# The maximum of attention as a row of its product, and a first section that starts with x and spreads dt*u by TensorE

## The reference

```python
# selective scan, per direction: u, dt (T x 256), B, C (T x 16)
dA = exp(dt[t, :, None] * A)
h  = dA * h + (dt[t] * u[t])[:, None] * B[t][None, :]
y[t] = einsum("ds,s->d", h, C[t])
# attention, 8 heads on 2 latent groups of 32, causal
p = softmax(q @ k.T * 128**-0.5 + mask)
```

## Time and profile before

| | us |
|---|---|
| median of 3 runs (1987.96 to 1991.94) | 1990.47 |
| profiled execution | 1983.65 |
| its span | 1981.8 |
| PE busy in the span | 1660.5 (84%) |
| DVE busy | 1547.1 (78%) |
| ACT busy | 1120.8 (57%) |
| POOL busy | 754.8 (38%) |

### The profile page before, as it was taken

How to read it: one execution, slowest core, us unless ns; L and a number is a source line. 1 busy time by engine, 2 the same in 40 slices (tenths; PEclk the granted TensorE clock), 3 DMA queues, 4 the chain that set the end, 5 groups by cost and what they waited for, 6 DMA issues and landing times.

```text
span 1981.8 us, 26962 instructions
## 1 busy us (share of the span) xinstructions
PE 1660.5 (84%) x8352; PEld 768.2 (39%) x8352; DVE 1547.1 (78%) x2173; ACT 1120.8 (57%) x1555; POOL 754.8 (38%) x601
## 2 busy tenths in 40 slices
PE   2434487889997999889997899889998999989988
PEld 0210123344443445344443345344443445434545
DVE  1999899869995899769995899869996999641404
ACT  2445387358744786458744786458744785433232
POOL 0345555324533355324533355324533445310102
PEclk8655699899999999899999999999999999989999
DMA  7999999657955687657955787657955686500000
GB/s 197 228 221 225 227 230 210 150 135 181 230 133 141 158 216 178 156 123 183 231 131 140 159 214 181 156 126 181 232 132 141 165 209 184 130 0 0 6 1 6
DMA packets 107915, 309.48 MB, mean 156 GB/s; under 512 B 15970, under 2 KB 32244, under 8 KB 107764
## 3 DMA queue, kind: packets, MB, share of 16 engines
q1 hardware_dynamic: 93556, 279.32, 59.5%
q10 hardware_dynamic: 14208, 28.32, 4.4%
HBM read 287.67 MB, written 19.92 MB: 155 GB/s over the span
## 4 chain that ended last, share of the span: by engine, by line
PE 36%; DVE 21%; ACT 21%; issue 12%; DMA 5%; ACTq 2%; DVEq 1%; SPq 1%; POOL 0%; POOLq 0%
PE ps_pair L698 8%; PE ps_pair L795 7%; DVE sb_hst L1263 7%; ACT L919 6%; PE ps_pair L854 5%; DMA sb_ring<-spread_dram 5%; PE ps_pair L783 4%; PE ps_pair L874 3%; PE ps_pair L651 3%; ACT sb_ring L950 3%; ACT sb_mix L1099 3%; DVE sb_dd L1241 2%; DVE ps_in L1255 2%; DVE sb_nmax L1404 2%; PE ps_pair L798 2%
## 5 line engine op out<-in xcount | busy, mean ns | idle before, releaser
L1532 POOL TENSOR_TENSOR sb_hc<-sb_hst,sb_crep 128x512 f32<-128x512 f32 x512 | 659.3, 1294 | 990.0 <-DVE sb_hst L1263 617.1
L1263 DVE TENSOR_TENSOR_SCAN sb_hst<-sb_ring,ps_in 128x512 f32<-128x512 f32 x512 | 620.5, 1212 | 21.2 <-ACT sb_ring L950 13.2
L950 ACT ACTIVATE sb_ring<-sb_ring,sb_A 128x512 f32<-128x512 f32 x512 | 345.2, 713 | 227.0 <-DMA sb_ring<-spread_dram 99.5
L1255 DVE TENSOR_TENSOR ps_in<-sb_ring,ps_brow 128x512 f32<-128x512 f32 x512 | 354.3, 692 | 22.1 <-DMA sb_ring<-spread_dram 4.7
L854 PE MATMUL ps_pair<-sb_mix,sb_ew 128*128 128x512 f32 x512 | 251.3, 625 | 19.8 <-ACT sb_h L1065 9.4
L919 ACT ACT_TABLE_LOAD x193 | 247.6, 1283 | 7.3 <-DVE sb_xd L1314 3.2
L633 PE MATMUL ps_y<-sb_hc,sb_const 128*32 128x512 f32 x1024 | 154.2, 677 | 83.0 <-POOL sb_hc L1532 59.4
L795 PE MATMUL ps_pair<-sb_g,sb_h 128*128 128x512 f32 x320 | 170.5, 658 | 23.4 <-DVE sb_dd L1243 11.1
L783 PE MATMUL ps_pair<-sb_h,sb_g 128*128 128x512 f32 (+3 forms) x512 | 165.4, 452 | 6.5 <-DVE sb_nmax L1404 3.2
L854 PEld LDWEIGHTS ps_pair<-sb_mix,sb_ew 128*128 128x128 f32 x512 | 96.0, 198 | 156.7 <-issue 87.1
L874 PEld LDWEIGHTS ps_pair<-sb_ew,sb_eh 128*128 128x128 f32 x1024 | 120.6, 192 | 37.3 <-issue 13.6
(11 more groups left out here) (219 smaller groups left out, 2037.9 us busy)
## 6 DMA issues: line engine op xcount, KB each, us to landing
sb_ring<-spread_dram SPq DMA_DIRECT2D x512, 512.0 KB, 5.6
spread_dram<-sb_dd ACTq DMA_DIRECT2D x32, 512.0 KB, 3.0
sb_brep<-cut_dram ACTq DMA_DIRECT2D x16, 256.0 KB, 3.8
sb_crep<-cut_dram ACTq DMA_DIRECT2D x16, 256.0 KB, 4.2
sb_xtok<-in_L_attn_x_dram SPq DMA_DIRECT2D x8, 256.0 KB, 5.1
sb_ew<-in_L_ffn_w_dram SPq DMA_DIRECT2D x2, 1024.0 KB, 8.5
out_dram<-sb_yy ACTq DMA_DIRECT2D x8, 256.0 KB, 2.3
sb_h<-in_L_ffn_h_w_dram SPq DMA_DIRECT2D x1, 1024.0 KB, 7.0
```

The lines of the kernel that those rows point to most:

```text
L950: act.activation(ring[:, n % RING, 0, :], ring[:, n % RING, 0, :], ACT.Exp, scale=A[d][:, g:g + 1]).then_inc(sem["dA"], 1)
L1255: dve.tensor_tensor(ps_in[n % 2][:], ring[:, n % RING, 1, :], ps_brow[:], ALU.mult).then_inc(sem["dbu"], 1)
L1263: dve.tensor_tensor_scan(hst[:, HST_SLOT[n], :], ring[:, n % RING, 0, :], ps_in[n % 2][:], 0.0, ALU.mult, ALU.add).then_inc(sem["scan"], 1)
L1532: pool.tensor_tensor(hc[:, n % 6, :], hst[:, HST_SLOT[n], :], crep[n // NU][:], ALU.mult).then_inc(sem["hc"], 1)
```

## The change

There are three parts, and all written-out orders are new.

**Attention.** The split into bf16 parts, `pick` and the products of line 798 go. `nmax` becomes a zeroed 128-column tile whose columns 0, 32, 64, 96 hold the maxima, in fp32; PE turns it with eight fp32 transposes into the two banks of `ps_pair[0]`, and ACT copies four single lines of it (1 x 1024 each) into a zero-key row of the queries, opposite to a line of ones (four copies of 1 x 512) in `kz`. The queries exist twice for that (`qAB`), one copy for each half. The score product of a round then contains the minus-maximum.

**The start.** x is SP's first load, then 12 loads of first need; the raising of the semaphores comes behind them; nine loads (`ones`: the backward direction and the mask) and 26 later ones follow. The 3 MB of expert weights and the gate's are issued in SECOND, one load after every fourth ring load.

**FIRST.** ACT copies dt*u to `duk`, and PE spreads it to 128 partitions by a 0/1 matrix, one product a unit, into one of g0 to g3; `drive` reads it from there, and B from SBUF. The ring's loads carry the dt half alone, 256 KB. ACT copies ten of the turned weights instead of DVE, and the turned weights use all four banks.

```diff
-            for name in PER:
-                sp.sem_inc(sem[name], first(name))
             with nc.allow_non_contiguous_dma(reason="per-channel vectors, once"):
+                sp.dma_start(xtok[:], a["x"][0:1]....).then_inc(sem["x_in"], 16)
+                for dst, src in loads[:-3]:
+                    sp.dma_start(dst, src).then_inc(w_in, 16)
                 sp.wait_ge(w_zero, 1)
-                for dst, src in loads:
+                for dst, src in loads[-3:]:
                     sp.dma_start(dst, src).then_inc(w_in, 16)
+                for name in PER:
+                    sp.sem_inc(sem[name], first(name))
+                for dst, src in ones:
+                    sp.dma_start(dst, src).then_inc(w_one, 16)
...
+            def spreads(at, tab):
+                row, claim = at(0), claim_of(at, tab)
+                for n in range(UNITS):
+                    hf, j, q = n // 16, n % 16 // 4, n % 4
+                    o = claim(f"du{n}")
+                    pe.wait_ge(sem["copied"], row("copied", hf + 1))
+                    rows = slice(32 * q, 32 * q + 32)
+                    pe.matmul(o[:], sel[rows, j, :], duk[rows, hf % 2, :], start=True, stop=True).then_inc(sem["spread"], 1)
+                    yield
...
                     for hf, (t, j) in enumerate(units):
-                        pe.matmul(ps_pair[0][:, hf, :], kz[:, 2 * k + hf, j * P:(j + 1) * P],
-                                  qT[:, TILES[hf].index(t), :, :], start=True, stop=False)
-                    for hf, (t, j) in enumerate(units):
-                        ins = pe.matmul(ps_pair[0][:, hf, :], pick[...].broadcast_to([P, P]), mT[...],
-                                        start=False, stop=(j < t))
+                        ins = pe.matmul(ps_pair[0][:, hf, :], kz[:, 2 * k + hf, j * P:(j + 1) * P],
+                                        qAB[hf][:, TILES[hf].index(t), :, :], start=True, stop=(j < t))
...
-                        ins = pe.transpose(o[:, tl, r, :], nsplit[:, tl, r, :, :]...., identb[:])
+                        ins = pe.transpose(ps_pair[0][:, tl, r * P:(r + 1) * P], nmax[:, tl, r, :], ident)
...
+                    if keep:
+                        act.wait_ge(sem["spread"], row("spread", 16 * hf - 16 if hf >= 2 else 0))
+                        act.activation(duk[:, hf % 2, :], dd[:, 1, :], ACT.Copy).then_inc(sem["copied"], 1)
...
-                    act.activation(qT[:, :, 2 * half:2 * half + 2, :]....
+                    for q in qAB:
+                        act.activation(q[:, :, 2 * half:2 * half + 2, :]....
...
-                act.activation(mT, full("mT")....
+                act.wait_ge(sem["full"], row("full", REST_INDEX[f"s{MAXIMA - 1}"] + 1))
+                for g in range(2 * KV):
+                    line = slice(LAT * PARTNER[g], LAT * PARTNER[g] + 1)
+                    ins = act.activation(kz[line, g, :], ones[line, 0:1].broadcast_to([1, T]), ACT.Copy)
+                ins.then_inc(sem["kone"], 1)
+                full("mT")
+                for g in range(2 * KV):
+                    line = slice(LAT * PARTNER[g], LAT * PARTNER[g] + 1)
+                    act.activation(qAB[g % 2][line]...., ps_pair[0][line], ACT.Copy).then_inc(sem["mT"], 1)
```

255 lines of the change are left out of this document (142 added, 113 removed).

## The result

The changed kernel is slower: 2000.34 us median of 4 runs (1998.76 to 2002.45) against 1989.22 of the kernel before on the same chip, a ratio of 1.0055 (95% interval 1.0037 to 1.0072). Forecast were 1946 us and a range of 1912 to 1976. The profiled execution took 1998.86 us with a span of 1996.8, 15.0 us more than the span before.

What follows compares the result with a forecast made beforehand. DVE was taken to bound FIRST (96% busy); in a loop pass no engine was full, PE nearest. Start -9.6, FIRST -3.3, SECOND -3, passes -22.5, FINAL and FLUSH -6 sum to -44.4: median 1946 us, range 1912 to 1976.

Steps and rivals of the forecast that it cites:

- table switches -3.1: Loop pass: six of 27 ACT table switches fewer, 7.7 us of ACT at a chain share of 0.41, -3.1 us.
- DVE's moved work -2: Loop pass: eight more half-units and the next head's convolution fill DVE's idle time in attention, -2 us (0 to -5).
- the ones at 0: Loop pass: ACT's four lines of ones, about 2.2 us, run beside DVE's last maximum and PE's transposes: 0.
- the expert loads of SECOND at +2: SECOND: 3.1 MB of expert weights among the ring's loads, 13.8 us of DMA, taken as +2 us.
- Start, -9.6: Start: x reaches PE 6.9 us earlier and the `spread` write takes 2.7 us less, so B is copied about 46.1.
- FIRST, -3.3: FIRST: DVE loses 6.7 us of weight copies to ACT and gains 3.4 us of idle time, -3.3 us.
- so it should rise: FIRST: PE, kept busy nearly all the time by the spread products, should get a clock above 0.75.
- half clock: Rival, chance 0.07: PE stays at the half level in FIRST, 190 instead of 162.6 us there, kernel 1973 us.
- A pass, -4.5: Each loop pass: attention, table switch, DVE and `dt1` terms sum to -4.5 us, five times that -22.5.
- `dt1` at the edge +2.5: End of a loop pass: `dt1` as last step costs between 0 and +5.5 us, taken as +2.5.
- FINAL and FLUSH, -6: End sections: FINAL -4 us with six switches fewer and no `dt1` at its end, FLUSH -2 from attention's terms.
- the edge of the pass: Rival, chance 0.12: `dt1` whole before the loop's jump, PE out of banks waits, pass +3.6 us, kernel 1995 us.

Runs made afterwards that it cites:

- e4: The changed kernel's start, FIRST and late expert loads, with the attention operations and steady strings of the kernel before: 1978.1 us, ratio 0.9953.
- e7: As e4, with the 11 expert loads issued among the ring loads of FIRST instead of SECOND: 1970.8 us, ratio 0.9916.
- e2: The changed kernel with the steady sections' old strings of steps from the kernel before: 1986.9 us, ratio 0.9995.
- e1: The kernel before, operations and start untouched, with the steady sections' new strings of steps: 2039.6 us, ratio 1.0243.
- e8: As e2, with only the next head's dt1 moved from attention's second round to behind var5 at the section's end: 2006.8 us, ratio 1.0098.
- e3: The changed kernel with one step of DVE's string moved, the second yT ahead of dt0 instead of behind it: 1992.3 us, ratio 1.0016.
- e12: The changed kernel with four expert steps put ahead of the queries' projection and two ahead of the first score product: 2012.3 us, ratio 1.0119.
- e10: The changed kernel with the next head's dt1 ahead of ao, and DVE's yT step ahead of dt0 as in e3: 2021.9 us, ratio 1.0180.
- e13: The changed kernel with the next head's last eleven steps at their places in the old strings: 2133.2 us, ratio 1.0733.
- e9: The changed kernel without ACT's lines of ones and three of its four line copies, leaving out part of the computation: 1985.3 us, ratio 0.9989.
- e5: The changed kernel with two of ACT's four lines of ones and two of its four line copies given to DVE: 2024.0 us, ratio 1.0180.

## Why the prediction was wrong

In short: the forecast of -44.4 us came out as +15.0 in the trace, and 50 of the 59 us between them lie in the passes, FINAL and FLUSH. The steps that failed are the pass's terms for the order (table switches -3.1, DVE's moved work -2, the yT step and six expert steps at nothing, `dt1` too low), the ones at 0, and the expert loads of SECOND at +2.

**Start, -9.6: right in sum**, -10.8 in the trace, with some luck in its terms. PE's transposes of x came 9.2 us earlier and not 6.9, above all since the first issue took 0.46 us where 2.05 were counted. The head from there to the `spread` write took 20.7 us instead of 24.6, for which the forecast had no term and no run gives a reason; the write held ACT 1.9 us less. The second dt step is 5.6 us, as forecast, but behind it DVE now prepares weights for 4.3 us (40.61 to 44.86) before it copies B, work that stood behind that copy before (56.98 to 61.1).

**FIRST, -3.3: right in size**, -1.9, by other terms: DVE lost 11.2 us of work and not 6.7, of which some 4 are that preparation, and its idle time rose by 9.3 us and not 3.4. Start and FIRST together don't depend on that border, -12.7 for -12.9. The clock was to be over 0.75 and was 0.59, although PE was busy for 85% of the section, and the step that failed there is "so it should rise": in 20 us with PE busy without a break the granted clock stayed at 0.50.

```profile
120.00:140.00 20.00, 19.90 (x38) 5.09 (x36) 19.62 (x26) 8.19 (x13) 10.19 (x8) 0.50 0.38 133
```

The rival "half clock" had its condition fulfilled and its price not, because PE took 80 us for the spread and not 116. The rows of three bursts show why (count = instructions, two for a spread product):

```profile
54.08 2.07 PE L673 MATMUL ps_pair<-sb_ea,sb_xn 32*128 32x512 f32 x2 [0.74 <-DVE ps_in L1323]
...
58.99 2.08 PE L673 MATMUL ps_pair<-sb_ea,sb_xn 32*128 32x512 f32 x6
...
69.47 2.15 PE L673 MATMUL ps_pair<-sb_ea,sb_xn 32*128 32x512 f32 x4 [3.83 <-DVE ps_in L1323]
```

The granted clock was 0.50 in all three windows. Two instructions alone took 2.07 us; six and four took 2.08 and 2.15. Products in different strips of 32 rows lay beside each other. This is the rule of the Trainium skill that the forecast had named without counting on it (TensorE: Matmul & The Clock Gate, "Measured speedup vs the span model"); the rows agree with it in kind, with two and three products in the time of one where it says 3.07 for four.

**SECOND, -3: wrong sign**, +5.7. The failed step is "against that 3.1 MB of expert weights ... I take +2": by e4 and e7 the loads cost 7.3 us, of the 13.8 worked out as pure transfer. They met the ring at its fullest: the forecast had gone by 0.79, the mean DMA share of the whole section, and e4's first quarter of it stood at 0.98; the earlier trace rows had shown 0.94 for 240 to 260 us. The -2 for a warmer clock didn't come either: the mean was 0.90, beside 0.92 before.

**A pass, -4.5: wrong**, +2.0 to +2.6 in four passes and +7.3 in the fifth, 3.3 in the mean. Its terms one by one:
- `pick` -4.3: right. e2's rounds are 3.8 us shorter, the changed kernel's 6.7 shorter than e1's.
- copies +2.8: right, 3.1. Split -0.9 and transposes +0.5: their lengths were right, but in e2 neither stood on the path, since ACT was waiting for the head's step meanwhile.
- the lines of ones, taken at 0 with "+2 if ACT comes to them late": this was the case, +2.5 in the old order. With it the new attention is a loss of some 1 us a section in the old order where -1.9 was summed (e2 less e4: +8.8 us). This step failed by itself, without the new strings.
- table loads -3.1 and DVE's moved work -2: the loads did leave the chain, 14 to 7.4 us, and no time followed. e1, which has all of this and the old attention, is 52 us slower. The step that failed is the reading of a share of the chain as a gain. No run takes the switches out alone, so what they are worth stays open; that another chain lay just behind theirs is my reading of the two chains.
- `dt1` at the edge +2.5: low, 4.0 by e8 in the old order and within its bounds, by the wait that it names (ACT back 6.2 us later, PE out of banks) and the half clock behind that wait. In the changed kernel the edge itself is 3.3 us longer.
- at nothing: DVE's yT behind dt0 (`->ao` +5.8; e3 gives back 2.6 of it, 8 us in the kernel), and six expert steps between q and s15 (+8.8 there against -11.6 in x3 to q; e12, which moves them back, is slower still).

**FINAL and FLUSH, -6: wrong**, +5.3 by B's copy. Cut at x3 they are 12.1 us longer, FINAL 2.0, FLUSH 9.9 (192.0 for 182.1), TAIL 0.2; in FINAL B's copy now stands 6.6 us behind x3 where it stood just ahead of it, and this border puts 6.8 us of the loss into the fifth pass. FLUSH has no scan and no head. With the new attention in the old order it is 184.0 (e2), so 8 of the 9.9 us are the order's: q to s15 is 10.3 us longer, x3 to q only 2.6 shorter. It isn't the place of the six expert steps alone, since e12 has FLUSH at 194.3.

The rival that came nearest is the edge of the pass, 1995 us at a chance of 0.12. Its mechanism was real and its price, 5.5 us a pass, a little too high; with e8's 20 us it accounts for less than half of the 50 that the passes, FINAL and FLUSH lost against the forecast. That its 1995 us lie near the 2000 measured is in part luck.

What stays open: which steps of the new strings cost the rest. Moving dt1 alone into the old order costs 20 us, the new order as a whole 13, so if prices added, which they didn't elsewhere, other placements in it would gain some 7. e3 undid one pair of steps and gained 8 us; three other attempts to undo parts (e10, e12, e13) all ended slower, and the runs name no further single step.

## What to carry to other kernels

Don't add the prices of edits that share a hand-written order: e4, e2, e1 and the changed kernel show the same attention edit at +8.8 and -30 us. A share of the critical chain bounds a gain and doesn't predict it; look up how long before its need the next input was ready (2.3 us for POOL's product here, and e9 gained 1.9). Work moved off a serial engine didn't pay in e5, where the engine that took it was feeding the very next wait.
